# A cross-attention and routed-FFN layer on one core: the order of each engine's steps written out over the whole program, and TensorE's constant products laid anew

## What is computed

```python
x = x + tanh(g_xattn[0]) * xattn(layernorm(x), ctx, ...)      # (8, 512, 256)
x = x + tanh(g_ffn[0]) * ffn(layernorm(x), ...)

def xattn(x_text, x_vision, ...):                              # 4 heads of 32
    scores = einsum('bthd,bghd->bhtg', Q, K) / sqrt(32)        # (8, 4, 512, 1024)
    topv, topi = top_k(scores, 32);  probs = softmax(topv)
    attn_mean = zeros.at[..., topi].set(probs).mean(axis=heads)
    c_t = attn_mean @ (x_vision @ Wv)
    x = layernorm(x_text) * (1 + g * scale_in) + g * shift_in  # scale, shift from c_t @ W_film_in
    y = s4d(x, ...)                                            # a long convolution over the 512 rows
    y = y * (1 + g * scale_out) + g * shift_out                # from c_t @ W_film_out
    xt = x_text + y
    xt = xt + gelu(layernorm(xt) @ W1 + b1) @ W2 + b2
    return layernorm(xt)

def ffn(x, ...):                                               # 8 experts, the best one for each row
    score = sigmoid(max(x @ gate_w));  e = argmax(x @ gate_w)
    return swiglu(x, shared) + swiglu_e(x * score)
```

## Time and profile before

| what | value |
|---|---|
| time, median of 3 runs | 1715.34 us (1712.01 to 1718.7) |
| span of the profiled execution | 1709.8 us |
| PE busy | 1512.3 us (88%) |
| DVE busy | 1382.8 us (81%) |
| POOL busy | 1152.1 us (67%) |
| ACT busy | 1135.8 us (66%) |
| constant products (L1946) | 277.9 us of PE's busy time, 1048 records |
| mean granted clock of TensorE | 0.955 of full speed |

### The profile page before, as it was taken

How to read it: one execution, slowest core, us unless ns; L and a number is a source line. 1 busy time by engine, 2 the same in 40 slices (tenths; PEclk the granted TensorE clock), 3 DMA queues, 4 the chain that set the end, 5 groups by cost and what they waited for, 6 DMA issues and landing times.

```text
span 1709.8 us, 22306 instructions
## 1 busy us (share of the span) xinstructions
PE 1512.3 (88%) x7299; PEld 1119.8 (65%) x7307; DVE 1382.8 (81%) x2241; ACT 1135.8 (66%) x2069; POOL 1152.1 (67%) x1267
## 2 busy tenths in 40 slices
PE   5887878798978897889999999999999899999996
PEld 3454655565656564667776777776776667667896
DVE  7798979997999899988898898889898999344321
ACT  3589955786578667866887678866886578322442
POOL 1498956757875887689768986798579858501322
PEclk8897989897989998999999999999999999999998
DMA  7200130002100210123313231322232112483431
GB/s 220 69 4 4 24 102 19 25 19 62 31 25 20 62 31 25 31 68 97 97 49 91 72 87 49 102 72 62 71 96 63 50 56 59 141 278 96 94 51 22
DMA packets 97223, 115.26 MB, mean 67 GB/s; under 512 B 17840, under 2 KB 74168, under 8 KB 96964
## 3 DMA queue, kind: packets, MB, share of 16 engines
q1 hardware_dynamic: 85348, 100.32, 20.2%
q0 software_dynamic: 11760, 13.52, 5.2%
HBM read 75.48 MB, written 19.58 MB: 56 GB/s over the span
## 4 chain that ended last, share of the span: by engine, by line
PE 36%; DVE 26%; ACT 16%; POOL 13%; issue 7%; DMA 1%; SPq 1%; POOLq 0%; DVEq 0%
DVE R L1500 8%; DVE ZB L1504 6%; PE PS L2371 4%; POOL ZB L779 3%; PE PS L2224 3%; DVE ZB L1496 3%; ACT ZB L1076 3%; PE PS L2248 3%; PE PS L1946 3%; DVE R L1456 2%; ACT R L1082 2%; PE PS L2176 2%; PE PS L1996 2%; PE PS L2177 2%; DVE R L1492 2%
## 5 line engine op out<-in xcount | busy, mean ns | idle before, releaser
L1500 DVE MAX8 R<-ZB 128x8 f32<-128x1024 f32 x384 | 471.0, 1227 | 10.3
L1504 DVE MATCH_REPLACE8 ZB<-R,ZB 128x1024 f32<-128x1024 f32 x256 | 309.5, 1209 | 0.0
L1946 PE MATMUL PS<-R 128*128 128x256 f32 x1048 | 277.9, 396 | 14.1 <-ACT R L1079 10.7
L779 POOL TENSOR_TENSOR ZB<-ZB 128x1024 f32<-128x1024 f32 x95 | 230.0, 2421 | 85.7 <-ACT ZB L1076 85.5
L1079 ACT ACTIVATE R<-PS 128x512 f32<-128x512 f32 (+6 forms) x404 | 172.4, 464 | 130.6 <-PE PS L2186 30.3
L1946 PEld LDWEIGHTS PS<-R 128*128 128x128 f32 x1048 | 198.6, 198 | 60.7 <-issue 17.0
L781 POOL TENSOR_TENSOR ZB<-ZB 128x1024 f32<-128x1024 f32 x95 | 224.2, 2360 | 7.5
L1492 DVE MAX8 R<-PS 128x8 f32<-128x1024 f32 x128 | 156.0, 1219 | 27.0 <-PE PS L1969 26.9
L1076 ACT ACTIVATE R<-R 128x32 f32<-128x32 f32 (+2 forms) x356 | 96.9, 273 | 96.8 <-DVE R L1500 28.2
L1496 DVE MATCH_REPLACE8 ZB<-R,PS 128x1024 f32<-128x1024 f32 x128 | 155.5, 1215 | 0.0
L1076 ACT ACTIVATE ZB<-ZB,R 128x1024 f32<-128x1024 f32 x128 | 147.1, 1149 | 4.2
(11 more groups left out here) (284 smaller groups left out, 3123.6 us busy)
## 6 DMA issues: line engine op xcount, KB each, us to landing
ZR<-ZR SPq DMA_DIRECT2D x96, 128.0 KB
ZB<-in_L_ffn_rt_gate SPq DMA_DIRECT2D x21, 512.0 KB, 4.2
ZB<-in_L_ffn_rt_up SPq DMA_DIRECT2D x21, 512.0 KB, 5.3
ZB<-in_L_ffn_rt_down SPq DMA_DIRECT2D x21, 512.0 KB, 4.6
R<-in_x SPq DMA_DIRECT2D x16, 512.0 KB, 4.2
ZB<-in_ctx SPq DMA_DIRECT2D x8, 768.0 KB, 4.9
R<-xs_d SPq DMA_DIRECT2D x39, 128.5 KB, 2.1
out<-R SPq DMA_DIRECT2D x32, 128.0 KB, 2.7
```

Of the source, the lines that this page charges most:

```text
L779: pool.tensor_tensor(e, e, w, ALU.mult).then_inc(s.g_att, 1)
L1500: vec.max(ml[:, 8 * r:8 * r + 8], w).then_inc(s_tk[n % 2], 1)
L1504: vec.match_replace(w, ml[:, 8 * r:8 * r + 8], w, NEG).then_inc(s_tk[n % 2], 1)
L1946: pe.matmul(q_bank(*key)[:, 0:256], ident, warm, start=True, stop=True)
```

## The change

The due times and all their tables are gone. For each engine a string gives the whole order, one character a step, and the character names the generator that makes its next step (`weave(order, clock, *parts)`). The generators themselves, their waits, their instructions and their buffers are as before. A string `PE_WARM` gives beside each step of PE how many constant products stand ahead of it. The ring of banks is laid by walking PE's string, and a constant product goes to the bank of the next step in it. In the diff, cut to its core, stand one of the five strings' first lines and the new functions:

```diff
-def weave(*parts):
-    at = [next(p, None) for p in parts]
-    while any(s is not None for s in at):
-        k = min((s, i) for i, s in enumerate(at) if s is not None)[1]
-        at[k] = next(parts[k], None)
+PE_ORDER = (
+    "05333333333554455155544156155465415335516655515662251531665125251522551665335525166512555136633212166321555152"
...
+def weave(order, clock, *parts):
+    for p in parts:
+        next(p)
+    for c in order:
+        clock.step += 1
+        next(parts[int(c, 36)], None)
...
-            def keep_warm(count, key):
+            clock = Clock()
+
+            def keep_warm():
+                count, key = int(PE_WARM[clock.step]), NEXT_BANK[clock.step]
...
-                    yield tile_at(n) + at[0]
+                    yield
                     on.wait_ge(s.p_sc, n + 1)
```

More of the change, by code:

```diff
@@ new lines, with lay_ring @@
+PE_PARTS = ('setup', 'attention', 'finish', 'prep', 'weights', 'kernel_rows', 'kernel_values', 'post', 'film_out', 'ranks', 'shared', 'tiles', 'routed')
+Q, NEXT_BANK, SET_UP = {}, [], 42
+def lay_ring():
+    left, walk, taken, early = {k: iter(v) for k, v in ring_keys().items()}, [], [0] * 4, SET_UP
+    for part in PE_ORDER:
+        name = PE_PARTS[int(part, 36)]
+        key = next(left[name]) if name in left else None
+        walk.append(key)
+        if key:
+            bank = len(Q) % (2 if early else 4)
+            Q[key] = (len(Q), bank, taken[bank])
+            taken[bank] += 1
+        early -= name == "kernel_rows"
+    following = None
+    for key in reversed(walk):
+        following = key or following
+        NEXT_BANK.insert(0, following)
@@ L736, in _ @@
             setup()
-            weave(inputs(), contexts(), queries(), keys(), kernel_rows(), late(), post(), tiles(), routed())
+            weave(SP_ORDER, Clock(), inputs(), contexts(), queries(), keys(), kernel_rows(), late(), post(), tiles(), routed())
         @block.gpsimd
@@ L1058, in routed @@
                 pool.drain()
-            weave(attention(), kernel_rows(), prep(), keys(), weights(), post(), shared(), tables(), tiles(), routed())
+            weave(POOL_ORDER, Clock(), attention(), kernel_rows(), prep(), keys(), weights(), post(), shared(), tables(), tiles(), routed())
         @block.scalar
```

681 lines of the change are left out of this document (298 added, 383 removed), and 10 rows, old and new, of tables (DVE_TOP, POST_AT).

## The result

The changed kernel takes **1688.1 us** (median of 4 runs, 1686.4 to 1688.9) against 1716.9 (1712.0 to 1718.7) for the kernel before: a ratio of 0.9835, with a 95% interval of 0.982 to 0.985. The forecast was 1659 us. The sign was right and the range held the time, but of the 56 us that the forecast took off (48 + 8 + 5 - 5), 28.8 came, about half. The profiled execution after spans 1686.6 us.

The account below looks back on a forecast made before the run. No engine alone bounds the kernel; DVE is nearest to full, with PE's excess holding it up in frames 4 to 6. 1709.8 - 48 - 8 - 5 + 5 = 1654, plus 5.5 to the median: 1659 us; range 1608 to 1712.

Parts of the forecast that it names:

- Setup: Before head 0: the first rounding ahead of the weight folding, the second behind head 0's first steps; 8 us less, bounds 0 to 9.
- The frames by PE's excess: Eight frames: PE's surplus of work over DVE's across eight heads counted as DVE waiting; its fall was to save 48 us.
- lower bound: Eight frames: no gain at all, if DVE's waits are due to its rhythm with ACT and POOL alone.
- The 49 us for 109 products: Frames 4 to 6: PE time saved by removing 109 constant products, at 0.45 us each.
- in frame 0 DVE has more work than PE throughout: Frame 0: no excess of PE's work over DVE's was counted there in the old order.
- stay whole: Eight frames: DVE's 1242.8 us of busy time would not change, making DVE the next engine to be late.
- The test named in advance: Frames 4 to 6: staying at 177 us with PE busy 150 would show that PE's excess was not the cause.
- rival 1: Whole kernel: fewer constant products let PE's granted clock fall, costing some 20 us; 1679 us, chance 0.11.
- rival 2: Whole kernel: PE's excess is no cause; only the removed products' share of the chain gains, 19 us; 1696 us, chance 0.14.
- After the last head: End of kernel: 22 of 31 constant products go, 5 us less; the 18 last tiles keep their rhythm, 0.
- New waits: Frames: heads stand closer in DVE's order; nine distances under 3 us cost 0.5 us each, 5 us back.
- rival 4: 28 heads with distances under 5 us: first maxima wait 4.4 us each; 1777 us, 1736 at two thirds; chance 0.18.

Follow-up runs that it names:

- new_old_products: The changed kernel's order with the old 524 constant products, each ahead of the same step as in the kernel before: 1806.5 us, ratio 1.0557.
- gaps_filled: New order to head 32, old to 64, then new, PE's last shared-expert steps before the last tiles; 203 constant products added where PE waited: 1704.5 us.
- old_thinned: The kernel before with only the constant products of heads 64 to 111 (frames 4 to 6) thinned from 184 to 75: 1717.2 us, ratio 1.0022.
- old_no_products: The kernel before, in its old order, with all 524 constant products left out: 1749.3 us, ratio 1.0204.
- new_to_head_32: Every engine in the new order up to head 32, then the old order of what is left; products by part: 1686.0 us, ratio 0.9855.

## Why the prediction was right in its sign and wrong in its main step

**Setup (-8 forecast, -10.5 measured).** The mechanism named is in the trace: the rounding starts 0.64 us after its product and not 6.85. The size was beyond the bound of 9 us, and no run changed this place alone. With the new order but more products in the setup (new_old_products, gaps_filled) head 0 came at 63.4 and 63.3 us instead of 58.7, so products' places have a share in it.

**The frames by PE's excess (-48 forecast, -22.9 measured with the new waits in it).** This is the step that failed, in two ways. The sum took "every microsecond of excess is one of waiting" and put 44 us at the four borders of the tile frames; frames 4 to 6 gave 8.2, and frame 3, whose excess was to fall from 16.7 to 5.7, became 7.6 longer. In the trace of before, all of VectorE's waits for PE in frames 4 to 6 are 24.1 us, so 44 could not come from there. old_thinned and old_no_products take the excess away without touching the order (26.6 and 33.9 us less on PE in these frames), and the frames come out 3.0 and 10.9 us longer in sum. The prediction's lower bound, "nothing", was the nearer one there; its condition, that DVE waits for ACT and POOL alone, is not what the trace shows, since 24.1 us of its waits are for PE, and they stay when PE's load falls. The 49 us for 109 products were too many as well: taken out alone they shortened PE's busy time by 26.6. (The "good fifth" of constant products in these frames is 93 of 511 us by the trace, a little under a fifth.) And "in frame 0 DVE has more work than PE throughout" led to no gain in frame 0, where the largest came (-13.1): PE had less work, and DVE still waited for it, 6.8 us for one head whose keys came late and 6.1 us for the filter. An account of loads over eight heads cannot see which step stands ahead of which, nor a transfer. Nor did DVE's work "stay whole": between the first maxima of head 0 and the last head it is 7 us less (1234.1 to 1226.9), for a reason that was not looked for.

**The test named in advance pointed this way but was not met as written.** "If frames 4 to 6 stay at 177 with PE at 150, the excess was not the cause": they took 173 to 180. PE was busy 157 to 163 us and not 144 to 152, though, in part by the clock, which fell from 0.99 to between 0.94 and 0.97; how large that part is was not measured. What speaks plainest is old_thinned, where nothing but the products changed.

**The clock (rival 1, 1679 us).** It came 9 us short of the time, and the clock did fall, from 0.955 to 0.936 in all. How much of the missing 28 us that is, no run shows. Leaving all products out costs 31 to 35 us net, with the clock down by 0.056 and 0.094. What the rival did not see is that the products removed and the clock they held nearly cancel each other: thinning 109 products in frames 4 to 6 changed the time by 0.2%. And new_to_head_32, with frames 4 to 6 in the old order at a clock of 1.00, has them at 181.2, 176.1 and 175.7 us, so a full clock does not shorten them to 167.

**Only the products count (rival 2, 1696 us).** Refuted: with all of them out of both kernels the order is still worth 30.5 us.

**After the last head (-5 forecast, +10.2 measured).** "The 18 last tiles have the same steps in the same rhythm: 0" was wrong. PE's rhythm was the same, but POOL's writes behind it are serial, and they started 33 us behind the first product instead of 10, with four shared-expert steps moved in among the tiles. Moving those steps back gave 6 of the 15 us by the two traces' lengths (22 us from the first product to the first write); the other 9 were not taken apart.

**New waits (+5 forecast) and rival 4 (1736 to 1777 us).** The first maxima wait 15.3 us for scores over the heads, less than the 26.9 before. VectorE's waits after, from the first head to the last:

```profile
DVE R L1433 <- ACT R L995: 19.3, 28, 1.7
DVE ZB L1414 <- POOL ZB L697: 15.6, 12, 3.0
DVE R L1410 <- PE PS L1889: 15.3, 14, 3.9
DVE R L1579 <- PE PS L2190: 11.1, 7, 2.3
DVE R L1634 <- PE PS L2130: 9.3, 5, 3.6
```

The short distances between heads did not hurt. What is new is the wait of L1634 in `post` (9.3 us; none before); that of L1579 was there (L1661 before: 11.9).

**What stays open.** What holds frames 4 to 6 at 173 to 180 us, with DVE busy 155 to 157 and every engine with slack. Frame 0 has about the same work on DVE, ACT and POOL and takes 164 us in the new order, so the sum of loads does not say it; the routed tiles are what these frames have and frame 0 has not, but no run took them apart from PE's load. Nor is it shown which engine's order makes the early gain: the trace points to SP's for 5.6 us of it (head 16's wait, 6.8 to 1.2), but no run changed one engine's order alone, and none cut between setup and frame 0.

## What to carry to other kernels

Before an engine's surplus of work is booked as waiting, ask which wait names it in the trace: here the gain stood in VectorE's waits in frame 0 (10.0 and 6.1 us), and in frames 4 to 6 the rows that name PE came to 24.1 us, about half of what was booked, and did not shrink with PE's load. Then follow the wait one step further: the longest of them was PE's own wait for a transfer. A product that only keeps the clock up is best added where PE waits for something other than the place that the product writes; ahead of a wait for its own bank it runs behind that wait. When steps move near the end, follow the serial queue (here accumulating writes of 4.5 us each), not only the busiest engine.

## What was not expected of the hardware

That idle moments of PE are so dear in a kernel where PE is only 80 to 88% busy: without constant products the granted clock fell from 0.955 to 0.861 in the old order and from 0.936 to 0.88 in the new one, and the kernels took 34.8 and about 31 us longer with 106 and 78 us less work on PE. And that it does not go on in a straight line: another 203 products raised the clock by 0.011 only in the profiled executions (0.945 to 0.956), by 0.018 by the runs' medians.
